# Cross attention and FP4 feed-forward block on one core: attention products in strips of 32 rows, and the hidden tile quantized in one piece a step later

## The reference

```python
x = x + attention(layernorm(x), ctx, mask)      # 16 heads of 32, 77 keys, biases in all four projections
x = x + fp4_linear(silu(fp4_linear(n, w_gate)) * fp4_linear(n, w_up), w_down)   # n = layernorm(x)

def fp4_quant_dequant(x):                       # blocks of 16 along the last dim
    scale = maximum(max(abs(xb)) / 6.0, 1e-12)
    xn = xb / scale
    q = GRID[searchsorted(MID, abs(xn))] * sign(xn) * scale   # 0, 0.5, 1, 1.5, 2, 3, 4, 6

def fp4_linear(x, w):
    return einsum('bsk,nk->bsn', fp4_quant_dequant(x), fp4_quant_dequant(w))
```

## Time and profile before

| | |
|---|---|
| median of 3 runs | 2224.2 us (2221.6 to 2224.77) |
| the profiled execution, its own time | 2219.91 us |
| span of its trace | 2218.1 us |
| mean granted TensorE clock | 0.971 |
| TensorE matmul busy | 2063.4 us (93%) |
| VectorE busy | 1888.9 us (85%) |
| ScalarE busy | 1175.3 us (53%) |
| GpSimd busy | 365.5 us (16%) |
| DMA, mean share of 16 engines | 50.7% for the queue that does nearly all |

### The profile page before, as it was taken

How to read it: one execution, slowest core, us unless ns; L and a number is a source line. 1 busy time by engine, 2 the same in 40 slices (tenths; PEclk the granted TensorE clock), 3 DMA queues, 4 the chain that set the end, 5 groups by cost and what they waited for, 6 DMA issues and landing times.

```text
span 2218.1 us, 45247 instructions
## 1 busy us (share of the span) xinstructions
PE 2063.4 (93%) x15744; PEld 1330.7 (60%) x15744; DVE 1888.9 (85%) x3380; ACT 1175.3 (53%) x2617; POOL 365.5 (16%) x523
## 2 busy tenths in 40 slices
PE   6335999999999999999999999999999999999998
PEld 4224566666666666666666666666666666666654
DVE  7777888889888888888888988898888888888875
ACT  5444555555555555555555555555555555555531
POOL 4543111111111111111111111111111111111100
PEclk9677999999999999999999999999999999999999
DMA  5333455554555455545555555545555555455542
GB/s 168 81 85 66 104 110 121 121 114 102 121 126 122 99 116 124 119 105 112 120 125 115 107 121 120 118 98 121 122 119 108 117 120 123 107 110 121 118 89 59
DMA packets 667573, 248.06 MB, mean 112 GB/s; under 512 B 619950, under 2 KB 620462, under 8 KB 667542
## 3 DMA queue, kind: packets, MB, share of 16 engines
q1 hardware_dynamic: 665958, 247.67, 50.7%
q10 hardware_dynamic: 1584, 0.01, 0.0%
HBM read 65.97 MB, written 34.82 MB: 45 GB/s over the span
## 4 chain that ended last, share of the span: by engine, by line
DVE 51%; PE 13%; issue 11%; POOL 9%; DMA 9%; ACT 5%; DVEq 1%; SPq 0%; ACTq 0%; POOLq 0%; another core or an unknown queue 0%
PE psum L543 10%; DMA t_room<-halves 9%; DVE h_room L888 5%; DVE h_sc L868 5%; DVE h_room L894 5%; DVE halves L856 4%; POOL ln_rstd L511 3%; DVE h_room L1042 3%; DVE h_room L898 2%; DVE h_room L902 2%; ACT q_room L825 2%; DVE h_sc L884 2%; POOL h_room L484 2%; ACT h_room L846 2%; DVE q_room L1028 2%
## 5 line engine op out<-in xcount | busy, mean ns | idle before, releaser
L614 PE MATMUL psum<-wguT,t_room 128*128 128x352 bf16 x6144 | 948.0, 313 | 2.3 <-DVE h_room L1042 1.8
L614 PEld LDWEIGHTS psum<-wguT,t_room 128*128 128x128 bf16 x6144 | 598.7, 98 | 329.0 <-DVE h_room L1042 2.1
L543 PE MATMUL psum<-wdT,ph_room 128*128 128x512 bf16 x2112 | 479.1, 380 | 5.5 <-DVE io_room L1074 5.2
L543 PEld LDWEIGHTS psum<-wdT,ph_room 128*128 128x128 bf16 x2112 | 207.1, 98 | 240.2 <-issue 9.0
L509 POOL TENSOR_TENSOR ln_var_eps<-ln_mean_var,eps 128x1 f32<-128x1 f32 x128 | 54.1, 422 | 1681.8 <-DVE ln_mean_var L1013 869.1
L766 ACT ACTIVATE silu_g<-psum 128x352 f32<-128x352 f32 x256 | 118.5, 463 | 323.4 <-PE psum L614 322.5
L772 ACT ACTIVATE probs<-psum,neg_max 128x77 f32<-128x77 f32 x1024 | 233.8, 339 | 20.5 <-DVE neg_max L1047 20.5
L543 PE MATMUL psum<-woT,t_room 128*128 128x512 bf16 x768 | 181.1, 386 | 24.0 <-DMA t_room<-halves 23.9
L543 PEld LDWEIGHTS psum<-t_room,wqT 128*128 128x128 bf16 x3072 | 180.4, 99 | 16.4 <-DVE wguT L856 1.8
L794 ACT ACTIVATE t_room<-psum,bq_col 128x128 bf16<-128x128 f32 x256 | 72.9, 368 | 220.2 <-PE psum L543 220.2
L697 ACT ACTIVATE h_sq<-h_room 128x640 bf16<-128x640 f32 (+3 forms) x158 | 121.2, 767 | 124.7 <-DVE h_room L888 117.1
(11 more groups left out here) (101 smaller groups left out, 2773.1 us busy)
## 6 DMA issues: line engine op xcount, KB each, us to landing
io_room<-in_x_dram SPq DMA_DIRECT2D x128, 256.0 KB, 2.8
x_scratch<-x_new SPq DMA_DIRECT2D x64, 256.0 KB, 2.5
x_cur<-x_scratch SPq DMA_DIRECT2D x64, 256.0 KB, 2.8
out_dram<-io_room SPq DMA_DIRECT2D x64, 256.0 KB, 2.1
t_room<-halves SPq DMA_TRANSPOSE x192, 3.1
raw<-in_L_ffn_w_down_dram SPq DMA_DIRECT2D x4, 704.0 KB, 4.3
raw<-in_L_ffn_w_gate_dram SPq DMA_DIRECT2D x11, 256.0 KB, 2.7
raw<-in_L_ffn_w_up_dram SPq DMA_DIRECT2D x11, 256.0 KB, 2.9
```

Source lines behind the costliest of these rows:

```text
L543: ins = pe.matmul(dst, left(i), right(j), start=first and n == 0, stop=last and n == len(PRODUCTS) - 1)
L614: ins = pe.matmul(ps[:, 0:CW], xqT[:, i, kc, :], wguT[:, which, j, kc, cols], start=(kc == 0 and i == j), stop=(kc == KC - 1 and i == LO))
```

## The change

What it does, in the order of the diff:

- **Scores and P times V in strips.** A matmul now takes 32 rows of contraction (one head), at row 0, 32, 64 or 96, and each of the four strips writes a PSUM bank of its own, banks 2 to 5. Scores: four mask products of 308 columns first, then 48 matmuls of 77 columns. P times V: 144 matmuls of 33 columns. P times V moves to the front of the step, ahead of the query projection, and waits there also for chunk 2 of the tile before. Scores write the banks that P times V wrote, so they still wait for `o_ready`.
- **The hidden tile in one piece.** Quantization of all 1408 columns happens in the step behind (tile `d`), from its start to its end, with one transpose of 22 blocks, and the down product of 33 matmuls runs another step later (tile `e`), between chunks 1 and 2.
- **Quantization itself.** `divide` becomes one instruction with two multiplications that carries the factor for ties, so `result_scale` is gone from the tiles' quantization.
- **Orders.** VectorE's and ScalarE's steps are ordered anew, and so are SP's transposes. Probabilities are padded to 96 keys.

The rows of its block of code, cut to the core:

```diff
+        head_ps = bank[2:6]
+        score_ps = psum[:, 2:6, 0:GROUPS * KEYS].rearrange("p r (g k) -> p r g k", g=GROUPS)
+        pv_ps = psum[:, 2:6, 0:GROUPS * VW].rearrange("p r (g w) -> p r g w", g=GROUPS)
+        down_ps = bank[6]
...
+                if a is not None:
+                    pe.wait_ge(pT0_loaded, 16 * a + 16)
+                    pe.wait_ge(pT1_loaded, 16 * a + 16)
+                    if d is not None:
+                        pe.wait_ge(h_done, d * CHUNKS + 3)
+                    for g in range(GROUPS):
+                        for j in range(KJ):
+                            for s, t in PRODUCTS:
+                                for rows, ps in zip(quarter, head_ps):
+
+                                    ins = pe.matmul(ps[:, g * VW:(g + 1) * VW], pT[rows, g // 2, s, j, g % 2, :],
+                                                    v_cur[rows, t, g, j, 0:VW],
...
+                    for ps in head_ps:
+                        pe.matmul(ps[:, 0:GROUPS * KEYS].rearrange("p (g k) -> p g k", g=GROUPS), ident_b[:],
+                                  mask_b[:].unsqueeze(1).to_broadcast([P, GROUPS, KEYS]), start=True, stop=False)
+                    pe.wait_ge(qT_lo, n + 1)
...
+                                ins = pe.matmul(ps[:, g * KEYS:(g + 1) * KEYS], qT[rows, s, g, :], k_cur[rows, t, g, :],
...
-                if d is not None:
-                    pe.wait_ge(hA_loaded, 16 * d + 16)
-                    at_least(pe, out_ready, d)
-                    down_part(0).then_inc(downA_done, 1)
+                if e is not None:
+                    pe.wait_ge(hT_loaded, 16 * e + 16)
+                    at_least(pe, out_ready, e)
+                    for k in range(IC):
+                        ins = split_product(down_ps, lambda s: hT[:, s, k, :], lambda s: wdT[:, s, k, :],
+                                            k == 0, k == IC - 1)
+                    ins.then_inc(down_done, 1)
...
-                step_of(job, dve.tensor_tensor(blocks(job.val), blocks(job.src), spread(job.sc, 3, job.nb), ALU.mult),
-                        job.divided)
+                step_of(job, dve.scalar_tensor_tensor(blocks(job.val), blocks(job.src), TIES_DOWN, spread(job.sc, 2, job.nb),
+                                                      ALU.mult, ALU.mult), job.divided)
```

More of the change, by code:

```diff
@@ L75, in xattn_fp4_ffn_kernel @@
     GW = GH * KEYS
[L76 to L80, removed]
+    KJ = -(-KEYS // DK)
+    KW = KJ * DK
+    VW = DK + 1
+    V_LOADS = 16 * KJ * GH
     TILES = BATCH * SEQ // P
@@ L334, in _ @@
             sp.wait_ge(consts_done, 1)
-            for c, h, first, end in V_BLOCKS:
-                row = first - c * P
-                sp.dma_start(v_cur[row:row + end - first, c, HI, :, P + h], ones_b[0:end - first, 0:GROUPS],
-                             allow_slow_non_contiguous=True).then_inc(ones_loaded, 16)
             sp.wait_ge(kv_stored, 32)
@@ L400, in step @@
                 weave("first")
-                if d is not None:
-                    after(hB_lo, d + 1)
-                    after(down_done, d)
-                    transposed(hT[1].rearrange("p s k t -> p (s k) t"), h_h[1].rearrange("p s w -> p (s w)"), hB_loaded)
                 if keys is not None:
-                    after(s_ps, 2 * n + 2)
+                    after(s_ps, GH * n + GH)
                     load_keys(keys)
@@ L421, in step @@
                     transposed(xqT.rearrange("p s k t -> p (s k) t"), xq_h.rearrange("p s d -> p (s d)"), xqT_loaded)
-                if f is not None:
-                    after(hA_lo, f + 1)
-                    after(downA_done, f)
-                    transposed(hT[0].rearrange("p s k t -> p (s k) t"), h_h[0].rearrange("p s w -> p (s w)"), hA_loaded)
+                if e is not None:
+                    after(out_ready, e + 1)
+                    sp.dma_start(one(out_t, e), out_sb).then_inc(out_stored, 16)
             rows = iter(range(2, WOVEN + 2))
@@ L459, in _ @@
             own.did(pool.memset(ident[:], 0.0))
[L460 to L462 removed]
+            own.did(pool.memset(v_cur[:].rearrange("p s g j w -> p (s g j w)").bitcast(U32), 0))
+            own.did(pool.memset(probs[:], 0.0))
+            own.after()
+            own.did(pool.memset(v_cur[:, HI, :, :, DK], 1.0))
             own.did(pool.memset(ones_b[:], 1.0))
@@ L1115, in step @@
                 weave("end")
-                run(f, scales, ha, (h_done, f * CHUNKS + 2) if f is not None else None)
-                run(f, divide, ha)
+                run(d, half_low, h_h, hq, h_hi, h_lo, d)
+                run(a, half_low, xq_h, xq, xq_hi, xq_lo, a)
                 run(f, h_chunk, 2)
-                run(a, half_low, xq_h, xq, xq_hi, xq_lo, a)
-                run(f, first_round, ha)
-                run(f, second_round, ha)
-                run(f, rescale, ha)
+                run(e, tile_out)
                 run(f, h_chunk, 3)
-                run(f, half_low, h_h[0], hq[:, H_PARTS[0]], hA_hi, hA_lo, f)
                 own.restart()
```

273 lines of the change are left out of this document (123 added, 150 removed).

## The result

| | before | after |
|---|---|---|
| median | 2223.9 us (2221.6 to 2224.77, 4 runs) | 2303.4 us (2302.04 to 2303.84, 4 runs) |
| ratio | | 1.036 [1.034, 1.038] |
| span of the trace | 2218.1 us | 2302.1 us |
| mean granted clock | 0.971 | 0.964 |
| TensorE matmul busy | 2063.4 us (93%) | 1969.8 us (86%) |

The change makes the kernel 3.6% slower. The forecast was 2392 us. The sign was right and the time lies in the range, but the loss is 80 us where 172 was forecast.

A forecast was written before the change was run, and what follows sets the result against it. TensorE bounds the kernel before; afterwards a step is P times V 3.6 + VectorE/ScalarE chain 12.45 + rest 17.86 = 33.9 us. 60 steps 150 + first steps 3 + last steps 19 = 172 on 2219.9: 2392 us, range 2222 to 2560.

The forecast's parts named there:

- the chain to chunk 1: VectorE and ScalarE work in fixed order after P times V, until chunk 1 can start: 12.45 us.
- the price of the thin product: Each 33-column product in P times V takes 25 ns, so 144 take 3.6 us (bounds 0.6 and 8.0).
- the bound of 4.1 ns: Low bound per 33-column product: a quarter of its 16.3 ns stream, if four strips run fully at once.
- The scores: 48 products of 77 columns at 35 ns, 1.7 us (bounds 0.4 and 2.7), hidden behind the chain under 1.85 us.
- The sync queue: SP's 22-block transpose precedes the next gate and up operand, ending two to three us before need; faster P times V shrinks this.
- The clock: TensorE's granted clock in the steady part: under 0.95 would show the forecast wrong.
- the rival: TensorE's clock falls after new waits and thin work: 2.5 us more a step, 2560 us; chance 0.12.
- The ends: Steps outside the 60 full ones: 3 us more for steps 0 and 1, 19 for the last steps.
- The last tile: Quantized whole with nothing beside it, 14.6 us, then transpose 5, down products 9.9, output 3.5: 33 against 18.8.
- Faster* rival: Thin products at 6 and 12 ns, chunk 0 of `h` ready in time: step 29.9, 2146 us; chance 0.06.
- V + 4.6: End of the attention output's LO half on VectorE, 4.6 us after the product following P times V begins.
- four strips at once: P times V takes 0.6 us but counts as 0.85: step 31.15, 2222 us; chance 0.12.

The follow-up runs named there:

- strip_by_strip: The changed kernel with the strip as the outermost loop of P times V, so 36 products in a row on one strip: 2424.8 us, 1.091.
- gpsimd_early: The changed kernel with GpSimd's residual add moved ahead of the first norm's arithmetic, to the start of its step: 2252.8 us, 1.014.
- whole_alone: The changed kernel with the attention products as before, so only the one-piece quantization and the changed order: 2400.8 us, 1.081.
- strips_alone: The kernel before with scores and P times V in strips and everything else as it was: 2319.6 us, 1.045.
- both_edits: The changed kernel with chunk 0 of h ahead of the first round on VectorE and GpSimd's add at the start of its step: 2217.3 us, 0.998.
- and_sp_order: chains_shortened with the mask's load and the second norm's transpose ahead of the 22 blocks of h on the sync queue: 2160.5 us, 0.972.
- output_first: and_sp_order with the attention output's LO half ahead of the reduce over 1408 columns on VectorE: 2157.4 us, 0.971.
- output_transpose_first: output_first with the attention output's transpose ahead of the 22 blocks of h on the sync queue: 2132.1 us, 0.960.
- strips_alone_gpsimd_early: strips_alone with GpSimd's add moved to the start of its step: 2284.0 us, 1.028.
- chunk0_first: The changed kernel with chunk 0 of h ahead of the first round on VectorE: 2277.0 us, 1.025.
- chains_shortened: The changed kernel with GpSimd's add early, queries' LO half and chunk 0 earlier on VectorE, first norm and silu before ScalarE's square: 2316.6 us, 1.044.

## Why the prediction came out as it did

- **The frame held.** The step is P times V, then the chain to chunk 1, then the rest: 1.33 + 13.18 + 17.97 = 32.48 measured, 3.6 + 12.45 + 17.86 = 33.9 forecast. strip_by_strip, with the forecast's price of a product, gave 3.47 + 12.97 + 17.96 = 34.40. That a nanosecond more per product is "0.144 us in a step and 9 us in all" held too: 14.9 ns between the two orders of the loop are 121 us, 8.1 us each.
- **The step that failed is the price of the thin product**, "a load this time is as long as the stream it should hide behind, so I take 25 ns". That price is right for products in a row on one strip (24.1 ns; load and stream by the forecast's own working would be 28). But the diff's inner loop goes over the four strips, and there the streams of the strips overlap: 9.2 ns, 36.9 for a set of four, where one stream alone was put at 16.3. The forecast had the bound of 4.1 ns for this and put it aside with "each needs its own load". It is worth (3.6 - 1.33) x 60 = 136 us. The Trainium skill's page TensorEngine Tiling (Array Packing), Instruction Overhead, which I had set on my side, holds here for one strip only (24.1 ns, its 60 cycles being 25). The same page of the Trainium skill, Key Properties, says that different tiles can load and multiply in parallel, and the 9.2 ns agree. The Trainium skill's page TensorE: Matmul & The Clock Gate, Packing small matmuls, has strips start about 4 ns apart; 9.2 ns at 33 columns is nearer to that than to 25, but more than twice as much.
- **The scores** were forecast at 1.7 us and took 0.54 (1001.48 to 1002.02 in strip_by_strip's timeline), 11.3 ns a product. Being hidden behind the chain, this changed only the waits: 1.12 ahead of chunk 1, where 0.2 to 0.5 was forecast.
- **The chain was 0.73 too short**: "GpSimd's residual moves under other VectorE instructions ... I take nothing". It fell beside the LO half of the attention output, on the chain, and cost 0.88 us. The bounds had been 0 to 0.7. gpsimd_early takes it away and has 12.31 against the 12.45 forecast. It is worth 44 us.
- **The sync queue** was named, "this cover shrinks with a faster P times V", and it did: 0.83 us of wait ahead of chunk 0. In the changed kernel this is hidden in the chain and costs nothing by itself (without it, in whole_alone, the scores start as late), but as soon as the chain gets shorter it is the bound.
- **The clock** stayed at 1.00 in the steady part, as forecast; the variants with waits of over 2 us show that the rival was real.
- **The ends** were forecast at 22 and are 84.0 - 60 x 1.09 = 19. The last tile came out as forecast: from the end of its last chunk (2269.19) to its down product it is 20.2 us, of which TensorE idles 13.08, and 14.6 and a transpose of 5 were forecast; to the end of the span it is 32.9, with 33 forecast. The 3 us lie in other steps and weren't followed:

```profile
2289.39 9.42 PE L534 MATMUL psum<-wdT,ph_room 128*128 128x512 bf16 x32 [13.08 <-DMA ph_room<-h_room]
```

- **Slips in the working** that move the forecast by nothing: the chain decides in the *Faster* rival below 11.1 us, not 10.6 (2.68 + 3.58 + 0.53 + 1.15 + 0.6 + 2.60); the output's LO half ends at V + 4.4 by the terms given, not 4.6; 2.5 us more in each of 60 steps on top of 2392 is 2542, not the 2560 that became the top of the range.

The terms together: 172 - 136 + 44 + 7 (0.11 us a step behind chunk 1) - 3 = 84, which is the difference of the two spans.

The rival "four strips at once" was half right: 9.2 ns is nearer to its 4.1 than to 25. It was wrong in that it expected no loss: P times V takes 1.33 and not the 0.85 it counted, and it kept the 12.45 for the chain.

## What to carry to other kernels

Price a small matmul by what the next one does: on the same strip it took 24.1 ns from one to the next here, with four strips taking turns 9.2. When an operation is made one large piece instead of two, look for what stands behind it in the order of each engine and of the DMA queue; in the steady steps the cost of the larger piece was in that, and moving two transposes, one GpSimd instruction and a few small ones ahead of it turned 3.6% slower into 4.0% faster. And work taken off a busy engine is a gain only if the next operand comes sooner too; otherwise it comes back as a wait. Behind a long wait the clock may fall as well, and in strips_alone that was most of the loss, so look at steps with and without a fall apart before naming a cause.

## What was not expected of the hardware

- Interleaved over four strips of 32 rows, load and product of 33 columns take 9.2 ns and of 77 columns 11.3 ns; on one strip in a row, 33 columns take 24.1 ns.
- Going over from products of 128 rows to thin ones costs about 0.1 us: from chunk 2 to P times V it is 7.26 us in the changed kernel, and 7.16 from chunk 2 to the down product before.
- A GpSimd add of two 128x512 float32 operands (1.27 us) lengthened a VectorE instruction beside it from 0.69 to 1.57 us; in the kernel before from 0.96 to 1.67. The Trainium skill's GPSIMD Engine Reference, Specifications, has GpSimd share its SBUF interfaces with VectorE, with contention for VectorE instructions that have two SBUF inputs; both of these have two, and with the add moved away they took 0.68 and 0.96.
- One DMA transpose of 22 blocks keeps the sync queue for 3.3 us, one of 8 blocks for 1.24; what stands behind it is issued that much later.
- The granted clock against the waits in a step (over 500 to 2000 us): 1.00 where the regular waits were up to 1.7 us (the change, gpsimd_early, both_edits, and_sp_order, output_first, output_transpose_first), 0.97 to 0.98 where one was 2.0 to 2.5 (strips_alone, strips_alone_gpsimd_early, chunk0_first, whole_alone, chains_shortened), with stretches at 1.2 GHz right behind the wait in a part of the steps. The length of the wait alone doesn't decide: in chains_shortened the same 2.17 us was followed by 3.75 us for 24 products in one step and by 5.43 in the next. And in strip_by_strip the fall came behind 144 thin products on one strip at a time with no wait between, and in output_transpose_first twice behind waits of only 1.44 and 0.83 us ahead of the thin products. What decides is open.
